# Node scores from the front's projection, the block search in another order, and the last program's constants, first lists and first gathers begun in the edge tables

## What is computed

```
h = (x_flat @ W_gat).reshape(M, HEADS, NUM_EXPERTS)        # 4 heads x 4
a_src = (h * att_src).sum(-1)                              # one number per node and head
a_dst = (h * att_dst).sum(-1)
e = leaky_relu(a_src[src] + a_dst[dst], 0.2)
ee = exp(e - e_max[dst]);  alpha = ee / segment_sum(ee, dst)
agg = segment_sum(h[src] * alpha, dst) + b_gat
scores = layernorm(agg).reshape(M, HEADS, NUM_EXPERTS).mean(1)
```

## Time and profile before

| | us |
|---|---|
| device time, three runs | 3456.33, 3470.45, 3469.91 (median 3469.91) |
| the profiled execution: device time | 3460.26 |
| the profiled execution: span, first to last instruction | 3458.5 |
| programs 1, 2, 3, 4 in it (begin) | 0, 1241.7, 1280.6, 1337.7 |

### The profile page before, as it was taken

How to read it: one execution, slowest core, us unless ns; L and a number is a source line. 1 busy time by engine, 2 the same in 40 slices (tenths; PEclk the granted TensorE clock), 3 DMA queues, 4 the chain that set the end, 5 groups by cost and what they waited for, 6 DMA issues and landing times.

```text
span 3458.5 us, 48939 instructions
## 1 busy us (share of the span) xinstructions
PE 2574.0 (74%) x15405; PEld 1900.7 (55%) x15406; DVE 2453.2 (71%) x7195; ACT 1765.3 (51%) x3180; POOL 1156.7 (33%) x1205
## 2 busy tenths in 40 slices
PE   1788888888888851212888878788787888888899
PEld 0566666666666631112565656556565566566666
DVE  6788778877778754435677768677876777686774
ACT  0566656666666510112555455555555555555654
POOL 0000000000000005765565665656565655555200
PEclk7899999999999965555788988989888888888899
DMA  2011111111111013222333323232333233233300
GB/s 89 31 49 43 49 43 49 47 46 38 42 49 37 31 65 97 44 58 63 84 67 81 73 64 91 62 91 65 84 69 84 68 75 82 61 87 69 81 13 10
DMA packets 228556, 210.48 MB, mean 61 GB/s; under 512 B 70781, under 2 KB 160585, under 8 KB 227657
## 3 DMA queue, kind: packets, MB, share of 16 engines
q1 hardware_dynamic: 190008, 190.83, 18.6%
q0 software_dynamic: 37280, 14.38, 5.1%
q10 hardware_dynamic: 1008, 2.15, 0.2%
HBM read 159.49 MB, written 47.74 MB: 60 GB/s over the span
## 4 chain that ended last, share of the span: by engine, by line
DVE 26%; PE 15%; another core or an unknown queue 9%; issue 9%; ACT 1%; DVEq 1%; SPq 0%; DMA 0%; ACTq 0%
DVE keep_x L2190 7%; PE lay_b_y L1804 6%; PE lay_b_z L1795 5%; DVE lay_oht L2095 1%; DVE lay_hid L2116 1%; DVE lay_oh L2092 1%; PE lay_b_b L1846 1%; DVE lay_split L1079 1%; DVE lay_stats L2215 1%; DVE lay_split L1080 1%; DVE lay_split L1076 1%; PE lay_b_att L1771 1%; PE lay_b_g L1896 1%; DVE lay_look L1073 1%
## 5 line engine op out<-in xcount | busy, mean ns | idle before, releaser
L1757 POOL DMA_INDIRECT lay_got<-node_table,lay_idx x1152 | 1132.1, 983 | 761.9 <-issue 308.6
L1804 PEld LDWEIGHTS lay_b_y<-lay_w,lay_hid 128*128 128x128 f32 x4096 | 535.7, 205 | 154.9 <-issue 152.9
L1795 PE MATMUL lay_b_z<-lay_xin,lay_w 128*128 128x512 f32 x1024 | 577.2, 692 | 11.4 <-ACT lay_hid L1949 8.3
L1804 PE MATMUL lay_b_y<-lay_w,lay_hid 128*128 128x128 f32 x4096 | 546.7, 288 | 29.9 <-issue 27.3
L2190 DVE SCALAR_TENSOR_TENSOR keep_x<-lay_b_y,lay_gates,keep_x 128x128 f32<-128x128 f32 x1024 | 287.5, 343 | 376.7 <-remote 211.3
L1949 ACT ACTIVATE lay_hid<-lay_b_z,lay_b 128x512 f32<-128x512 f32 x512 | 328.8, 682 | 395.0 <-PE lay_b_z L1795 199.9
L885 POOL MEMSET find_no_src<- 128x9 int32 x1 | 0.1, 107 | 1239.8 <-POOLq L48 1239.8
L2037 ACT ACTIVATE lay_unused<-lay_hub_wide,lay_halves 128x1152 bf16<-128x1152 uint16 x256 | 320.3, 1251 | 133.7 <-DMA lay_hub_wide<-sorted_dst 111.3
L468 PE MATMUL front_b_h<-front_xt,front_m 128*128 128x512 f32 x512 | 272.8, 664 | 59.5 <-ACT front_act_m L578 30.9
L1795 PEld LDWEIGHTS lay_b_z<-lay_xin,lay_w 128*128 128x128 f32 x1024 | 201.0, 218 | 175.3 <-issue 153.1
L224 DVE TENSOR_TENSOR sort_keys<-sort_keys 128x1024 f32<-128x1024 f32 (+2 forms) x182 | 257.4, 1414 | 42.4 <-ACT sort_keys L546 39.9
(11 more groups left out here) (398 smaller groups left out, 4249.7 us busy)
## 6 DMA issues: line engine op xcount, KB each, us to landing
lay_wide<-sorted_dst SPq DMA_DIRECT2D x128, 288.0 KB
lay_hub_wide<-sorted_dst SPq DMA_DIRECT2D x128, 288.0 KB
made<-front_y SPq DMA_DIRECT2D x128, 256.0 KB, 2.0
lay_y<-made SPq DMA_DIRECT2D x32, 1024.0 KB
lay_got<-node_table,lay_idx POOLq DMA_INDIRECT x1152
front_adj<-in_adj SPq DMA_DIRECT2D x32, 256.0 KB, 3.0
keep_x<-in_x SPq DMA_DIRECT2D x32, 256.0 KB, 3.4
lay_adj<-in_adj SPq DMA_DIRECT2D x32, 256.0 KB
```

Of the source, the lines that this page charges most:

```text
L1757: pool.indirect_dma_start(out=got[:, b % RING, c, :], out_offset=None, in_=table, in_offset=bass.IndirectOffsetOnAxis(ap=idx[:, b % AHEAD, ...
L1795: pe.matmul(b_z[c][:, :], w1[:, e, P * c:P * c + P], flat(xin[g % 2][:, :, :]), start=True, stop=True).then_inc(z_done, 1)
L1804: mm = pe.matmul(b_y[n % 2][:, P * j:P * j + P], hid[n % 2][:, c, P * j:P * j + P], w2[:, e * HK + c, :], start=(c == 0), stop=(c == HK - 1))
```

## The change

Six edits, which the diff below shows cut to what matters:

1. **Projection.** `wg` has 24 columns. DVE fills columns 16 to 23 at the start of program 1 with `W_gat` times `att_src` and `att_dst`, summed for each head (four more DVE operations, two more weight loads, and the waits go from ten weights to twelve). `project` and the copy are 24 columns wide. Program 3's multiplications and sums of 2048 columns (L1344, L1345, L1347, L1348) and its two weight loads are gone; it begins with `top`.
2. **Block search.** In program 2 DVE no longer waits for the constants before its first operations; `below` comes before `src` and `dst_u`, and `row_of` before the count of valid keys and the keys aside.
3. **Order in program 3.** `rest_step` and `more_free` are raised at once; own messages and `hub_e` are computed between the rest loop and the more loop; `far` comes before `near`; `hub_row` is read by SP and not by ACT.
4. **Constants** of program 4 are made by POOL in program 3, right after the all-reduce.
5. **First lists.** SP issues `rows` of blocks 0 to 7, two windows and two hub windows at the start of program 3.
6. **First gathers.** POOL issues the nine gathers of block 0 at the end of program 3, behind the more loop.

```diff
+                    pe.matmul(b_p[:, TAB * j:TAB * j + TAB], xt[:, j, :], wg[:, :], start=True, stop=True)
...
+            for u in range(2):
+                gin.link(v.tensor_tensor(wg_att[:, :], wg[:, 0:HC], att[:, u, :], ALU.mult))
+                gin.link(v.tensor_reduce(wg[:, HC + HEADS * u:HC + HEADS * u + HEADS],
...
-            v.wait_ge(consts, 16)
             ints = bufs[1 - final][:, 0:cols].bitcast(I32)
             me.mark(v.tensor_single_scalar(ints, bufs[final][:, 0:cols].bitcast(I32), LOW_BITS, ALU.logical_shift_right))
+            me.wait()
+            me.link(v.tensor_scalar(cls[:, :], ints, -float(OFFSET), None, ALU.add))
+            me.link(v.tensor_reduce(row_top[:, :], cls[:, cols - LOOSE:cols], AX.X, ALU.max))
+            v.wait_ge(consts, 16)
+            v.tensor_scalar(below[:, :], bound_row[:, :], row_top[:, 0:1], None, ALU.is_gt)\
+                .then_inc(below_ready, 1)
             v.tensor_single_scalar(src[:, 0:cols], ...).then_inc(lists_ready, 1)
             v.tensor_copy(dst_u[:, :], cls[:, :]).then_inc(lists_ready, 1)
+            v.wait_ge(rows_summed, 1)
+            v.tensor_scalar(row_of[:, :], banks[0][:, 0:2 * blocks], iota_p[:, 0:1], None, ALU.is_equal)\
...
         def _(sp):      # edge_tables
-            for dst, src in ((att_src, "att_src"), (att_dst, "att_dst")):
+            for b in range(AHEAD):
+                at = first_at(sp, 0, b)
+                for dst, src in ((lay["idx"], sorted_src), (lay["to"], sorted_dst)):
+                    sp.dma_start(dst[:, b, :], rows_at(src, at)).then_inc(lay["rows_in"][b], 16)
+            for b in range(2):
+                sp.dma_start(lay["wide"][:, b, :], wide_at(first_at(sp, 0, b))).then_inc(lay["wide_in"][b], 16)
+            for b in range(2):
+                sp.dma_start(lay["hub_wide"][:, b, :], wide_at(first_at(sp, 1, b))).then_inc(...)
+            sp.wait_ge(table_out, 16)
+            sp.dma_start(hub_row[:, :], table[nodes - 1:nodes, :].broadcast_to([P, TAB])).then_inc(hub_in, 16)
...
             pool.partition_all_reduce(top_sb[:, :], top[:, :], P, bass.bass_isa.ReduceOp.max).then_inc(top_all, 1)
+            pool.memset(lay["ident"][:, :], 0.0).then_inc(lay_consts, 1)
+            pool.iota(lay["iota_b"][:, :], ...)
...
+            pool.wait_ge(lay_consts, 7)
+            pool.affine_select(out=lay["ident"][:, :], ...)
+            pool.affine_select(out=lay["least"][:, :, :], ...)
             pool.wait_ge(table_out, 16)
             pool.wait_ge(far_out, 16)
...
+            for b in range(1):
+                pool.wait_ge(lay["rows_in"][b], 32)
+                for c in range(GC):
+                    pool.indirect_dma_start(out=lay["got"][:, b, c, :], ..., in_=table, ...)
             pool.wait_ge(more_free, n + 1)
...
         def _(v):       # edge_tables
-            me.link(v.tensor_tensor(prod[:, :, :], h, over(att_src[:, :].unsqueeze(1), T3), ALU.mult))
-            me.link(v.tensor_reduce(near_e, ...))
             v.tensor_reduce(top[:, :], near_e.rearrange("p t h -> p h t"), AX.X, ALU.max).then_inc(top_ready, 1)
+            v.sem_inc(rest_step, 1)
+            v.sem_inc(more_free, 1)
...
-            for b in range(tiles):      # layers, gpsimd
+            for b in range(1, tiles):
```

More of the change, by code:

```diff
@@ L34 @@
 RING = 4
+AHEAD = 8
 PARTS = 3
@@ L455, in project @@
                 for j in range(TB):
[L456 removed]
+                    mm = pe.matmul(b_p[:, TAB * j:TAB * j + TAB], xt[:, j, :], wg[:, :], start=True, stop=True)
                 mm.then_inc(proj_done, 1)
@@ L1125, in edge_tables @@
         top_sb = s.sb("top_sb", [P, HEADS])
+        lay, n_gates = keep, keep["least"].shape[1]
         more_idx = s.sb("more_idx", [P, GC], I32)
@@ L1259, in _ @@
                 pool.sem_inc(turn, 1)
+            for b in range(1):
+                pool.wait_ge(lay["rows_in"][b], 32)
+                for c in range(GC):
+                    pool.indirect_dma_start(
+                        out=lay["got"][:, b, c, :], out_offset=None, in_=table,
+                        in_offset=bass.IndirectOffsetOnAxis(ap=lay["idx"][:, b, c:c + 1].bitcast(U32), axis=0))\
+                        .then_inc(lay["gathered"][b], 16)
             pool.wait_ge(more_free, n + 1)
@@ L1683, in store @@
                 sp.dma_start(ov[:, of(g), :], x[:, of(g), :]).then_inc(stored, 16)
-            for b in range(AHEAD):
-                rows(b)
-            window(0)
-            window(1)
-            hub_window(0)
-            hub_window(1)
             sp.dma_start(w1[:, :, :], w["W1"].rearrange("e d h -> d e h")).then_inc(weights, 16)
```

159 lines of the change are left out of this document (68 added, 91 removed).

## The result

| | before | after |
|---|---|---|
| device time, median | 3470.18 us (3456.33 to 3479.88, 4 runs) | 3434.99 us (3425.2 to 3442.81, 4 runs) |
| the profiled execution: device time, span | 3460.26, 3458.5 | 3435.44, 3433.7 |
| program 1, begin to end | 1241.7 | 1238.9 |
| program 2 | 38.8 | 33.7 |
| program 3 | 57.2 | 58.8 |

The ratio is 0.9901, 95% interval 0.9871 to 0.993: the changed kernel is 35 us faster by the medians, and 25 us by the two profiled executions. The forecast was 3442.8, with 3424 to 3465 as range; it holds.

A forecast was written before the change was run, and what follows sets the result against it. The stretch before the experts was taken as bound by POOL's chain of gathers and what precedes its first one. Terms +2.0 - 4.5 + 3.0 - 25.7 + 3.8 = -21.4 on 3464.2 gave 3442.8 us, range 3424 to 3465.

The forecast's parts named there:

- Program 1, +2.0: Program 1: added loads, four small DVE operations and a wider copy cost 2.0 us (0 to +3.5).
- Program 2, -4.5: Program 2: DVE starts without waiting for constants, row_of comes earlier; gain between 3.1 and 5.4 us, 4.5 taken.
- The step that was hedged: Program 2: DVE's early operations may hold POOL up, constants 2.3 us later; gain then 3.1 us, otherwise 5.4.
- Program 3, +3.0: Program 3: near and the rest come earlier, but block 0's gathers now end the program, making it 3.0 us longer.
- The two standings of about 7 us: Program 3: POOL stands 7.05 us before the all-reduce and again before the iota behind it, changing kinds of work.
- Program 4, -25.7 + 3.8: Program 4: block 1's first gather comes 25.7 us earlier; slower gathers of blocks 1 to 3 give 3.8 back.
- The give-back: Program 4: blocks 1 to 3 gather beside four more pairs of DVE's one-hots, 40.5 us instead of 36.7, +3.8.
- No load before the all-reduce: Rival, program 3: POOL does not stand before the all-reduce, near comes at S+4.7; -28, 3436 us; 15%.
- Engines standing while POOL gathers from its first instruction: Rival, program 4: other engines stand until blocks 1 to 3 are issued, lead at block 4 only 15.5; 3449 us; 13%.
- The lead given back in POOL's pauses: Rival, program 4: two more of POOL's longest full-ring waits for DVE, leaving a lead of 2; 3462 us; 12%.
- the slower case: Rival, program 4: five more full-ring pauses of 9.7 us, 48 more waiting less 21; +27, 3491 us; 8%.
- The parts doing less: Rival, programs 1 to 3: held-up constants, slow loads, far against windows, each at its bad end; -15.5, 3449 us; 7%.

The follow-up runs named there:

- x_pe_top: Changed kernel with POOL's all-reduce replaced by small steps of PE and DVE: 3164.2 us, 0.991 of before.
- x_consts_back: Changed kernel with edit 4 alone undone, so POOL makes program 4's constants at that program's start again: 3184.5 us.
- x_small_hots: Changed kernel with its sixteen pairs of large one-hots cut from 1024 to 128 columns each, PE's sums of them to an eighth: 3158.6 us.
- c_before: The kernel before, unchanged, profiled again on chip 2, where it takes 3193.5 or 3193.6 us.
- c_after: The changed kernel, unedited, on the same chip 2 as the kernel before: 3163.97 us, 0.9915 of before.
- x_pe_top_late: x_pe_top with POOL's large iota held back until DVE has made near and far: 3167.2 us, 0.9911 of before.
- x_fill: x_pe_top_late with four of block 0's gathers issued once the node table landed, and no POOL wait for the more round's last gather: 3155.5 us, 0.9882 of before.

## Why the prediction was right, point by point

**Program 1, +2.0: not to be seen.** The start cost is there: DVE's `eps_ident` 0.46 us later (29.02 against 28.56), the four operations 0.8, and the sort's first slice 1.3 later (30.77 against 29.48). But the program ended 2.8 us earlier. Over all executions it ended at 1241.7 and 1244.8 without edit 1, and between 1235.5 and 1244.4, 1241.0 on average, in eleven with it. Two terms of tenths were summed against a stage whose end moves by 9 us; whether +2.0 or nothing is true stays open.

**Program 2, -4.5: -5.1 and -5.2 in the profiles, 5.4 by undoing it.** The step that was hedged, POOL's constants held up by DVE, happened nearly in full: they came 2.2 us later (5.9 against 3.7; 2.3 was the bound), and `row_of` 8.5 us after the start and not 6.8. That the gain came out whole all the same is luck: the eight counts followed each other every 0.68 us (1253.65 to 1259.09), where 0.86 was taken, and that gives back 1.5 us. Two misses nearly cancel.

**Program 3, +3.0: +1.7.** The two standings of about 7 us were the heart of it, and x_pe_top and x_consts_back show that the reason holds: the all-reduce and the iotas each pay on a change. The size was off: 5.64 on the way there (7.05 taken), and the all-reduce itself took 0.39 and not 2.31. In the kernel before it ran beside one of DVE's multiplications of 2048 columns, which the change removes:

```profile
1289.69 2.29 DVE L1347 TENSOR_TENSOR att_prod<-edge_h,att_att_dst 128x2048 f32<-128x2048 f32 x1
```

So `near` came at 8.2 and not 11.5. Of these 3.3 us, 1.3 were left at the end of the program: `more` gathers beside DVE's own messages took up to 1.96 each, which the sum left out, and the change of programs took 2.7 us (1.5 taken).

**Program 4, -25.7 + 3.8: -32.0 and +7.4 by the clock on the first chip.** Block 1's first gather was 6.3 us earlier than forecast; 4.8 of that is program 1, which is scatter and so luck, 0.6 program 2, 1.3 program 3, less 0.4 that the first gather takes to begin. The give-back was mis-sized: blocks 1 to 3 took 44.1 us and not 40.5. The forecast let the eight large one-hots of block 0 run beside them besides the eight that did before. But 20 ran beside them and not 16, for DVE, whose messages of block 0 no longer wait for gathers, comes to block 3's as well. In the kernel before, DVE had stood in front of those, and block 3's gathers ran bare:

```profile
1404.28 1.22 DVE L2116 TENSOR_TENSOR lay_hid<-lay_iota_b,keep_hub_node 128x1024 bf16<-128x1024 bf16 x1 [7.91 <-remote]
```

On chip 2 nothing stood: 12 ran beside blocks 1 to 3 before and 20 after, and the give-back is 5.0 us (38.8 to 43.8). For eight more that is still above the 3.8 taken from block 0's gathers. x_small_hots gives the price of all sixteen pairs over seven blocks, 12.8 us.

**The total, -21.4: 35 us by the medians, 25 by the two profiled executions of the first chip, 27 by the ratio on chip 2 (1 - 0.9915 of 3194).** The sum counts 0.5 us twice: block 1's gather at 1338.4 already holds the +2.0 - 4.5 + 3.0 of the programs ahead, so the terms give -21.9, which is the lead that the forecast itself states at block 4. Measured by the clock that lead was 24.6 us. The forecast then said that it stays; on the first chip it grew to 33.7 at the first expert, as POOL paused less, which no term held. Behind the first expert nothing changed in the program, but that stretch takes 1802 and 1811 us on the first chip, and 1592 to 1609 in eleven executions on the others: a spread of 17 us whatever was edited, nearly as large as the gain. In the profiled pair it took 9 us back, in c_before and c_after it added 17 to a lead of 32. So the mechanism is shown by the milestones: leaving program 1 out, the forecast has 23.9 us, chip 2 shows 26.0 at the first expert and the first chip 30.9. That the time came within 8 us of the forecast is in part luck: the misses ahead of the first expert sum to 12 us in favour, and the forecast was put on 3464.2, 6 us under the median that the kernel before shows with its fourth run.

**The rivals.** No load before the all-reduce, that is, no standing of POOL there: fell, as POOL stood 5.64 us. Engines standing while POOL gathers from its first instruction: fell, since messages of block 0 came 10.2 us after block 1's first gather; the standing was there later, from block 7 on. The lead given back in POOL's pauses, and the slower case, both read off 1500 to 1620 us before: POOL's waits for DVE at the full ring, from block 1's gathers to the first expert (us in all, times, longest), first before, then after:

```profile
POOL lay_got L1757 <- DVE lay_split L1080: 37.4, 7, 9.7
```
```profile
POOL keep_got L1748 <- DVE lay_split L1088: 36.0, 6, 10.4
```

The waits did not grow, so neither happened. The parts doing less: in program 2 the hold-up went to its bad end, in the others nothing did by more than a few us.

## What to carry to other kernels

Count the start of a chain that one engine sets (here POOL's gathers), and what slows its first links: undoing the constants cost 16.6 us, while gathers moved ahead of a program's end gave back 4.1 of the 6.6 us of their lead, because DVE's large operations then met the next ones. When an operation moves, ask what ran beside it: the all-reduce took 2.31 us beside a large operation of DVE and 0.39 without it. Check that a gain which a start time already holds is not summed a second time. And where a stage behind the change scatters by as much as the gain, compare milestones in the trace from a common start.

## What the runs showed of the hardware

**Switching POOL's kind of work costs both ways.** An all-reduce behind ordinary instructions stood 5.6 to 6.3 us in eight executions, the first iota behind it 6.9 to 7.7 in seven of them, and 11.04 in the eighth, where SP's weights moved meanwhile. The memset behind the all-reduce (1280.00 us, 0.27) stood for nothing. In x_consts_back gathers came between the all-reduce and the iota, and the iota stood all the same. With no all-reduce in the program (x_pe_top, x_pe_top_late, x_fill), neither standing is there.

**POOL and DVE slow each other in some pairs of operations.** Beside one another a memset took 1.28 us (0.20 without DVE), a gather 1.96 (0.94), the large iota 3.77 (2.28), a DVE operation on 16 numbers 3.47 (0.22). The 4 by 4 operation of x_pe_top began behind the iota and ended with it (1275.00 and 1274.98). Not every pair does it: six operations of DVE on 128x1 numbers that began and ended beside the same iota in the changed kernel took 0.14 or 0.15 us each, and the iota 2.28. The all-reduce took 2.31 in both traces of the kernel before, beside that multiplication, and 0.39 in all eight without it; nothing else was varied for it, so there the cause is argued. What decides which pairs are slowed was not shown.

**The engines' standings on the first chip have no cause that was found.** Timeline of the changed kernel on it, PE's look-up for block 8 and POOL around its pause:

```profile
1439.99 0.70 PE L1760 MATMUL lay_b_att<-keep_far_parts,lay_oht 128*128 128x12 bf16 x9 [0.77 <-issue]
...
1470.62 0.94 POOL L1748 DMA_INDIRECT keep_got<-node_table,keep_idx  x1 [0.30 <-issue]
...
1479.99 0.94 POOL L1748 DMA_INDIRECT keep_got<-node_table,keep_idx  x1 [8.42 <-DVE lay_split L1088]
```

Block 8's gathers were all issued by 1437.3, PE had looked up by 1440.7, and DVE began its messages at 1477.89, 6.3 us after POOL's last gather before the full ring. PE, ACT and DVE ran nothing in between. A backlog of the gathers' data is not the cause: 32 packets go with each gather (37280 on that queue in the whole execution, for 1165 indirect DMAs), and by 1441.0 the queue of the gathers had moved 2336 of them from 1331 on, more than the 2304 of blocks 1 to 8. Whether the signal that they had landed came late, the trace does not show. The other chips show none of this, with the same gathers at the same pace; there the kernel before is 277 us faster. So POOL's issuing alone does not hold the others; what differs on the first chip is open, as no experiment ran there.
